# A graph attention layer and a quantised feed-forward layer on one core: edge weights scattered directly, laid over a mask base made on chip

## What is computed

```
w = softplus(edge_type_weights)                      # four numbers
mask = full((N, N), -inf)
mask = mask.at[src, dst].set(w[edge_type - 1])
mask = mask.at[idx, idx].set(where(isneginf(diag), w[3], diag))
scores = einsum('hnd,hmd->hnm', q2, k2) * scale + mask[None]
attn = softmax(scores, axis=-1)
out = einsum('hnm,hmd->hnd', attn, v2) @ wo.T + bo
```

## Time and profile before

| | |
|---|---|
| median of three runs | 340.25 us (337.29 to 341.86) |
| the profiled execution | 339.55 us, of which the span of the trace is 337.6 us |
| TensorE busy | 324.9 us, 96% of the span |
| VectorE, ScalarE, GpSimd busy | 234.8, 182.4, 190.4 us |

### The profile page before, as it was taken

One profiled execution on the slowest core, in us unless ns is written; L12 is line 12 of the kernel. 1 busy time (PEld: TensorE's weight loads), 2 busy tenths in 40 slices (PEclk: granted clock), 3 DMA queues, 4 the chain that ended last, 5 costly groups with the idle time before them and its releaser, 6 DMA issues.

```text
span 337.6 us, 5993 instructions
## 1 busy us (share of the span) xinstructions
PE 324.9 (96%) x2086; PEld 299.0 (89%) x2086; DVE 234.8 (70%) x605; ACT 182.4 (54%) x333; POOL 190.4 (56%) x250
## 2 busy tenths in 40 slices
PE   5999999999999999999799999999999999999995
PEld 5899998878999999999799999999999978888864
DVE  4857887964085554459965979778797876497574
ACT  4824248372843333333147769577595866243572
POOL 6876667446786667489955393755627666100000
PEclk9999999999999999999799999999999999999999
DMA  7997346577053435643230332303113120000005
GB/s 254 371 397 274 122 129 192 183 233 240 7 165 134 128 102 159 217 181 99 90 124 17 112 102 86 124 2 125 61 67 112 57 85 0 0 2 0 2 0 188
DMA packets 17371, 41.72 MB, mean 124 GB/s; under 512 B 3536, under 2 KB 8000, under 8 KB 17344
## 3 DMA queue, kind: packets, MB, share of 16 engines
q1 hardware_dynamic: 14432, 38.87, 33.5%
q0 software_dynamic: 2064, 1.80, 1.9%
q10 hardware_dynamic: 848, 0.70, 0.6%
HBM read 37.99 MB, written 3.37 MB: 123 GB/s over the span
## 4 chain that ended last, share of the span: by engine, by line
PE 57%; DMA 16%; POOL 9%; issue 8%; DVE 7%; ACT 1%; POOLq 0%; DVEq 0%; ACTq 0%
PE PS L749 32%; DMA codes<-ecol,place 14%; POOL codes L436 6%; PE PS L906 5%; PE PS L894 5%; PE PS L882 4%; PE PS L730 3%; PE PS L1041 2%; DMA scratch<-codes 2%; DVE scratch L1304 2%; POOL ring L419 1%; DVE scratch L1303 1%; PE PS L1095 1%; PE PS L818 1%; PE PS L808 1%
## 5 line engine op out<-in xcount | busy, mean ns | idle before, releaser
L419 POOL TENSOR_TENSOR ring<-stage,ring 128x256 fp32r<-128x256 f32 x124 | 97.1, 819 | 38.7 <-ACT ring L502 37.6
L749 PE MATMUL PS<-XT,ring 128*128 128x384 f32 x528 | 93.9, 336 | 0.8 <-DVE QT L1206 0.5
L749 PEld LDWEIGHTS PS<-XT,ring 128*128 128x128 f32 x528 | 91.3, 188 | 1.5 <-issue 0.8
L436 POOL DMA_INDIRECT codes<-ecol,place x51 | 58.3, 1143 | 28.3 <-DMA codes<-ecol,place 16.5
L502 ACT ACTIVATE ring<-stage 128x1024 fp32r<-128x1024 f32 x52 | 54.3, 1056 | 7.0 <-PE PS L749 3.8
L607 ACT ACTIVATE scratch<-scratch,smx 128x384 f32<-128x384 f32 x48 | 28.9, 604 | 22.8 <-DVE smx L1326 22.8
L749 PE MATMUL PS<-QT,ring 128*128 128x384 f32 x192 | 37.2, 349 | 2.1 <-DVE Q L1313 2.1
L749 PEld LDWEIGHTS PS<-QT,ring 128*128 128x128 f32 x192 | 34.7, 196 | 2.7 <-issue 2.7
L1244 DVE TENSOR_TENSOR ring<-stage,ring 128x1024 fp32r<-128x1024 f32 x21 | 25.6, 1225 | 16.3 <-ACT ring L502 16.3
L749 PE MATMUL PS<-AT,ring 128*128 128x384 f32 x192 | 35.2, 338 | 0.0
L749 PEld LDWEIGHTS PS<-AT,ring 128*128 128x128 f32 x192 | 33.0, 188 | 1.5 <-issue 1.5
(11 more groups left out here) (199 smaller groups left out, 476.0 us busy)
## 6 DMA issues: line engine op xcount, KB each, us to landing
stage<-in_weights SPq DMA_DIRECT2D x56, 512.0 KB, 3.4
V<-in_w_gate_up SPq DMA_DIRECT2D x4, 512.0 KB, 3.6
scratch<-codes POOLq DMA_DIRECT2D x3, 576.0 KB, 5.9
X<-in_x SPq DMA_DIRECT2D x3, 512.0 KB, 5.0
out<-X SPq DMA_DIRECT2D x4, 384.0 KB, 2.6
codes<-scratch SPq DMA_DIRECT2D x2, 576.0 KB, 12.9
scratch<-in_w_gate_up SPq DMA_DIRECT2D x2, 512.0 KB, 5.2
V<-in_w_down SPq DMA_DIRECT2D x5, 176.0 KB, 3.7
```

What stands on the lines that cost most here:

```text
L419: ins = pool.tensor_tensor(ring[1][:, slot, piece], stage[:, slot % STAGE, piece], ring[0][:, slot, piece].bitcast(F32), ALU.subtract)
L436: pool.indirect_dma_start(codes[b].rearrange("(n a) -> n a", a=1), bass.IndirectOffsetOnAxis(ap=place[:, t:t + 1], axis=0), ecol[:, VAL, t ...
L749: ins = pe.matmul(outs, lhs[a], rhs[b], start=start and n == 0, stop=stop and n == 2, skip_group_check=True)
```

## The change

The tables are blanked with zeros alone, one broadcast transfer each, so that SyncE issues three transfers in place of nine. Edge values are now the final weights (softplus times 8, at least 1e-30), so that a nonzero bit pattern marks an edge. For that, ScalarE's exp and log move into steps 1 to 3 of the V stage, VectorE's two small operations behind step 5 of that stage (`kind_weights`), and GpSimd selects each edge's weight with four test-and-multiply operations and three additions (`edge_values`) between the low parts of chunks 8 and 9. The four operations that made the codes are gone. In the K stage, VectorE writes the mask's base behind K tile 1 (`edge_base`): -1e30 everywhere, the fourth kind's weight on the diagonal. Each table has its own semaphore when it comes back, and VectorE lays it over the base with one predicated copy (`edges_over`), behind K tiles 4, 5 and 6. The third table comes back into `PT[0][0]`.

```diff
@@ constants, areas @@
+LEAST_WEIGHT = 1e-30
+        tables = [scratch[:, 0:NT * N], scratch[:, NT * N:2 * NT * N],
+                  PT[0][0][:, :, :].rearrange("p t n -> p (t n)").bitcast(F32)]
+        mask_flat = scratch[:, 2 * NT * N:3 * NT * N]
@@ SyncE @@
-            for b in range(1, LISTS):
+            for b in range(LISTS):
                 sp.dma_start(codes[b].rearrange("(m p n) -> p m n", m=NT, p=P), blank.to_broadcast([P, NT, N])
                              ).then_inc(codes_blank[b], 16)
-            sp.wait_ge(diag_ready, 1)
-            for m in range(NT):
...
@@ GpSimd @@
-            chain.step(pool.tensor_scalar(ecol[:, TYP, :], ecol[:, TYP, :], 0.25, 1.0, ALU.mult, ALU.add))
-            for b in range(LISTS):
...
-            ins.then_inc(cols_ready, 1)
+            pool.sem_inc(cols_ready, 1)
+            def edge_values():
+                parts = (VAL, NEG, SPARE, SPARE + 1)
+                pool.wait_ge(kind_ready, 1)
+                for w, to in enumerate(parts):
+                    chain.link(pool.tensor_scalar(ecol[:, to, :], ecol[:, TYP, :], float(w), ew[:, 5, w:w + 1],
+                                                  ALU.is_equal, ALU.mult))
+                chain.join()
+                chain.link(pool.tensor_tensor(ecol[:, VAL, :], ecol[:, VAL, :], ecol[:, NEG, :], ALU.add))
+                chain.step(pool.tensor_tensor(ecol[:, SPARE, :], ecol[:, SPARE, :], ecol[:, SPARE + 1, :], ALU.add))
+                chain.step(pool.tensor_tensor(ecol[:, VAL, :], ecol[:, VAL, :], ecol[:, SPARE, :], ALU.add))
...
-            for c in range(CIV + 2):
+            for c in range(CIV + 1):
                 low(c, c % RING)
+            edge_values()
+            low(CIV + 1, (CIV + 1) % RING)
...
-            for b, area in enumerate((SM[0], SM[1], mask)):
+            for b in range(LISTS):
                 pool.wait_ge(scattered[b], 16 * PER_LIST)
-                pool.dma_start(area, codes[b].rearrange("(m p n) -> p m n", m=NT, p=P)).then_inc(code_back, 16)
+                pool.dma_start(tables[b].rearrange("p (m n) -> p m n", m=NT),
+                               codes[b].rearrange("(m p n) -> p m n", m=NT, p=P)).then_inc(code_back[b], 16)
@@ ScalarE, V stage (the same four lines go from before the Q stage) @@
+                if s == 1:
+                    chain.step(act.activation(ew[:, 1, :], ew[:, 0, :], ACT.Abs))
+                    chain.step(act.activation(ew[:, 2, :], ew[:, 1, :], ACT.Exp, scale=-1.0))
+                elif s == 2:
+                    act.activation(ew[:, 3, :], ew[:, 2, :], ACT.Ln, bias=1.0).then_inc(soft_in, 1)
+                elif s == 3:
+                    act.activation(clip[:, 1, :], clip[:, 0, :], ACT.Exp, scale=-1.0).then_inc(soft_in, 1)
@@ VectorE @@
-            dve.wait_ge(consts, 6)
-            dve.tensor_scalar(diag[:, :], ident[:, :], 1.75, None, ALU.mult).then_inc(diag_ready, 1)
...
+            def kind_weights():
+                dve.wait_ge(soft_in, 1)
+                chain.step(dve.scalar_tensor_tensor(ew[:, 4, :], ew[:, 0, :], 0.0, ew[:, 3, :], ALU.max, ALU.add))
+                dve.tensor_scalar(ew[:, 5, :], ew[:, 4, :], 1.0 / SCALE, LEAST_WEIGHT, ALU.mult, ALU.max
+                                  ).then_inc(kind_ready, 1)
...
+                if s == 5:
+                    kind_weights()
...
+            def edge_base():
+                for b in range(LISTS):
+                    dve.wait_ge(codes_blank[b], 16)
+                dve.wait_ge(kind_ready, 1)
+                chain.link(dve.tensor_scalar(diag[:, :], ident[:, :], 0.0, NO_EDGE, ALU.is_equal, ALU.mult))
+                chain.step(dve.memset(mask_flat, NO_EDGE))
+                for m in range(NT):
+                    chain.link(dve.scalar_tensor_tensor(mask[:, m, m * P:(m + 1) * P], ident[:, :], ew[:, 5, 3:4],
+                                                        diag[:, :], ALU.mult, ALU.add))
+                chain.join()
+
+            def edges_over(b):
+                dve.wait_ge(code_back[b], 16)
+                chain.step(dve.copy_predicated(mask_flat, tables[b].bitcast(I32), tables[b]))
+
             for s in range(5):
                 k_tile(s)
-
-            dve.wait_ge(code_back, 16 * LISTS)
-            chain.step(dve.tensor_tensor(mask, mask, SM[0], ALU.add))
+                if s == 1:
+                    edge_base()
+            edges_over(0)
             k_tile(5)
-            chain.step(dve.tensor_tensor(mask, mask, SM[1], ALU.add))
+            edges_over(1)
             k_tile(6)
-            kind = SM[0].bitcast(I32)
...
-            weight_of(0)
+            edges_over(2)
             k_tile(7)
-            weight_of(1)
-            weight_of(2)
...
             q_low(0)
-            weight_of(3)
             k_low(0)
```

More of the change, by code:

```diff
@@ L215, in gnn_ffn @@
         blank_ready = sem("blank_ready")
-        diag_ready = sem("diag_ready")
+        kind_ready = sem("kind_ready")
         codes_blank = [sem(f"codes_blank{b}") for b in range(LISTS)]
@@ L219, in gnn_ffn @@
         scattered = [sem(f"scattered{b}") for b in range(LISTS)]
-        code_back = sem("code_back")
+        code_back = [sem(f"code_back{b}") for b in range(LISTS)]
         pool_chain = sem("pool_chain")
@@ L396, in _ @@
                                base=-EC, pattern=[[-1, EC]], channel_multiplier=1).then_inc(rows_ready, 1)
-            SRC, DST, KEY, TYP, NEG, VAL = range(6)
+            SRC, DST, KEY, TYP, NEG, VAL, SPARE = range(7)
             pool.wait_ge(edges_in, 2 * 16)
@@ L434, in _ @@
                     else:
-                        pool.wait_ge(codes_blank[b], 16 * (1 if b else 3 * NT - 2))
+                        pool.wait_ge(codes_blank[b], 16)
                     pool.indirect_dma_start(codes[b].rearrange("(n a) -> n a", a=1),
@@ L583, in _ @@
                                        ).then_inc(acc_free, 1)
-            chain.step(act.activation(ew[:, 1, :], ew[:, 0, :], ACT.Abs))
-            chain.step(act.activation(ew[:, 2, :], ew[:, 1, :], ACT.Exp, scale=-1.0))
-            act.activation(ew[:, 3, :], ew[:, 2, :], ACT.Ln, bias=1.0).then_inc(soft_in, 1)
-            act.activation(clip[:, 1, :], clip[:, 0, :], ACT.Exp, scale=-1.0).then_inc(soft_in, 1)
             early(QT, CQ, BIAS_Q)
@@ L1276, in _ @@
             dve.wait_ge(soft_in, 2)
-            chain.step(dve.scalar_tensor_tensor(ew[:, 4, :], ew[:, 0, :], 0.0, ew[:, 3, :], ALU.max, ALU.add))
-            chain.step(dve.tensor_scalar(ew[:, 5, :], ew[:, 4, :], 1.0 / SCALE, None, ALU.mult))
             chain.step(dve.tensor_scalar(clip[:, 2, :], clip[:, 1, :], 1.0, None, ALU.add))
@@ L1288, in k_tile @@
                 tile_low(s + 16, s, s % 2, AT, s + BIAS_K)
+            def edge_base():
[11 more added lines that the diff above has]
+                chain.step(dve.copy_predicated(mask_flat, tables[b].bitcast(I32), tables[b]))
             for s in range(5):
                 k_tile(s)
-            dve.wait_ge(code_back, 16 * LISTS)
-            chain.step(dve.tensor_tensor(mask, mask, SM[0], ALU.add))
+                if s == 1:
+                    edge_base()
+            edges_over(0)
             k_tile(5)
-            chain.step(dve.tensor_tensor(mask, mask, SM[1], ALU.add))
+            edges_over(1)
             k_tile(6)
-            kind = SM[0].bitcast(I32)
-            chain.step(dve.tensor_scalar(kind, mask.bitcast(I32), 21, 3, ALU.logical_shift_right, ALU.bitwise_and))
-            chain.step(dve.tensor_scalar(mask, mask, 0.0, NO_EDGE, ALU.is_equal, ALU.mult))
-            def weight_of(w):
-                chain.step(dve.tensor_scalar(SM[1], kind, kinds[:, w:w + 1], ew[:, 5, w:w + 1], ALU.is_equal, ALU.mult))
-                chain.step(dve.tensor_tensor(mask, mask, SM[1], ALU.add))
-            weight_of(0)
+            edges_over(2)
             k_tile(7)
-            weight_of(1)
-            weight_of(2)
             def q_low(t):
```

13 lines of the change are left out of this document (2 added, 11 removed).

## The result

| | before | changed |
|---|---|---|
| median | 340.30 us (337.29 to 341.88, 6 runs) | 334.67 us (334.56 to 336.96, 6 runs) |
| the profiled execution | 339.55 us, span 337.6 us | 334.56 us, span 332.7 us |
| ratio of times | | 0.990, 95% interval 0.985 to 0.994 |

The forecast was 335.2 us. The ratio is taken over runs of the fast state alone; that of the two medians is 0.983. So the changed kernel is faster by 1.0% or by 1.7%, and both lie inside the 2% that the prediction called no difference.

What follows compares the result with a forecast made beforehand. TensorE, busy 96% of the span, was taken as the bound, so only its waits pay: -4.21 us at the K stage's end, clock included, and -0.5 at the Q tile, -4.7 together. Forecast 335.2 us, range 332.5 to 338.5.

Steps and rivals of the forecast that it cites:

- `q_low(0)`: End of the K stage: TensorE's wait on VectorE before chunk 34 goes, -2.14 us.
- K tile 5: K stage: its low part comes in time after the first copy, so TensorE's wait before chunk 31 goes, -0.33 us.
- The Q wait: Q stage: three table loads leave ScalarE's way to the first Q tile, so TensorE's wait there goes, -0.5 us.
- The clock: Chunk 34: the slow TensorE clock behind the idling goes with the wait, -1.74 us.
- The V stage: Softplus moved there: one ScalarE result 0.6 us late, cost to TensorE 0, at worst 0.2 us.
- The scatters: GpSimd's edge weights ahead of them: first scatter, and by assumption the last and the read-backs, 1.4 us later.
- The cover: K stage: 1.5 us to spare before chunk 31 would wait for late tables.
- GpSimd's pace: Low-part pieces beside the copies take 0.7 to 0.9 us each in place of 1.32; no cost counted.
- The sum: Whole kernel: -4.21 - 0.5 = -4.7 us.
- A: Larger gain, a late scatter chain having cost TensorE all its lateness before: 332 to 333.4 us, chance 0.18.
- B: A late first table makes TensorE wait at chunk 31, or GpSimd stays slow: 336.5 to 339 us, chance 0.16.
- C: Predicated copy far dearer than an addition, TensorE waits at chunks 31 to 34: 350 us, chance 0.02.

Runs made afterwards that it cites:

- (8): Kernel before without the third and fourth kinds' weight pairs in the mask, a shorter VectorE block: 335.85 us, ratio 0.994.
- (3): Changed kernel with five additions of 128x1152 put back behind K tile 7, ahead of `q_low(0)`: 338.36 us, one run.
- (1): Kernel before with only ScalarE's softplus and clip lines moved into the V stage: 337.44 us against 337.60, ratio 0.999.
- (4): Kernel before, nothing changed, traced again: 337.74 us, one run.
- experiment 2: Changed kernel, but VectorE waits for all three tables before its first copy: 339.38 us, ratio to the kernel before 0.998.
- experiment 6: Changed kernel, nothing changed, timed again on another chip: 334.37 us against 337.72 of the kernel before, ratio 0.990.
- 9: Kernel before with softplus and clip moved into the V stage and the third and fourth kinds' weights left out: 335.52 us, ratio 0.992.

## Why the prediction was right

*`q_low(0)`.* Forecast -2.14, measured -2.31 (3.21 - 0.90). Chunk 34 at 161.88, forecast 162.1. The cause is shown by three runs: the block shortened removes the wait (8), a block put back into the changed kernel makes it (3), and tables that came earlier leave it (1).

*K tile 5.* Forecast -0.33, measured -0.61. The copy was priced at 1.9 us; it took 1.82, 2.10 and 1.96. The first began at 145.80, inside 144.6 to 146, and K tile 5 at 147.66, forecast 147.9.

*The Q wait.* Forecast -0.5, measured -0.74. Both short waits cost 0.25 to 0.28 us more than the wait that TensorE's rows show. Part is in how I read the rows: a chunk's row is 4.32 us long, but the next chunk starts 4.16 us after it, so a wait counted from the end of a row is 0.16 us short. The other 0.12 is the chunk behind the wait: 154.47 - 150.19 = 4.28 us in place of 4.16. The same 0.16 is what `q_low(0)` gave above its forecast: TensorE could have had chunk 34 at 158.63 + 4.16 = 162.79, not at 162.95.

*The clock.* Forecast -1.74, measured -1.64. This term was priced rightly and read wrongly: the prediction counted it as given wherever the wait is. That it came in full is luck of the trace that was compared. Experiments 3 and 4 show waits of 2.51 and 1.70 us with no fall, the first trace and experiment 2 waits of 2.14 and 2.57 us with one. So the gain is 3.3 us against a run that kept its clock (337.7 - 334.4, experiment 6), and 5.6 by the medians of the first measurement (340.3 - 334.7), where four of six runs of the kernel before took over 340. The forecast of 4.7 lies between the two. On a chip where the kernel before keeps its clock the same reasoning would have been 1.4 us too high.

*The V stage.* Forecast 0, at worst 0.2; measured +0.45. The opening gives 0.06 of it (13.34 against 13.28), and the softplus itself nothing: the result of chunk 2, forecast 0.6 us late, was taken at 27.78 against 27.70. The rest is the new wait at line 790. TensorE in the kernel before and in the changed one:

```profile
73.82 0.51 PE L783 MATMUL PS<-turner,V 96*128 96x96 f16 x8
```

```profile
74.27 0.52 PE L790 MATMUL PS<-turner,V 96*128 96x96 f16 x8 [0.31 <-DVE V L1242]
```

and VectorE, which prepares these weights, in both:

```profile
70.61 1.22 DVE L1228 TENSOR_REDUCE fsc<-V 128x1 f32<-128x1024 f32 x1 [3.62 <-DMA V<-in_w_down]
```

```profile
71.06 1.22 DVE L1233 TENSOR_REDUCE fsc<-V 128x1 f32<-128x1024 f32 x1 [3.38 <-DMA V<-in_w_down]
```

VectorE waits for a load of feed-forward weights, which SyncE issued at 66.86 and 66.92. From issue to VectorE's start it took 3.75 us before and 4.14 in the changed kernel. In the 14 traces the wait at this line stands exactly in the five in which this took 4.13 to 4.52 us, and in none of the nine in which it took 3.40 to 3.93; the changed kernel has both (3.64 in experiment 6). So the forecast looked in the wrong place: it weighed ScalarE's results, and the cost came from a load. Whether the change makes that load slower stays open: all five are among the ten traces with the moved softplus. Four of these ten, experiments 1, 3 and 9 among them, also have a wait of 0.4 us at the keys' transposes, and none of the four without it.

*The scatters.* Forecast 1.4 us later, measured 2.0: `edge_values` took the 2.9 us and the wait 0.41 that were forecast, and chunk 9's low part took 3.28 us in place of 2.83. The first read-back is 3.0 us later than before, the third only 1.0. The cover took it all.

*GpSimd's pace.* Forecast 0.7 to 0.9 us a piece, measured 0.93, enough: no wait of TensorE on it before the scores.

*The sum.* -0.61 - 2.31 - 0.74 - 1.64 + 0.45 = -4.85, forecast -4.7. The short waits erred by 0.5 and `q_low(0)` by 0.2 one way, the V stage by 0.45 and the clock by 0.1 the other. That they cancel is luck; the waits, their places and what removes them were forecast.

*The rivals.* A gave a large gain to a late scatter chain. Its spread was real, and the traces give it another cause: the clock (4). The landing was the same in two traces whose times differ by 1.8 us (4), and an earlier one moved `q_low(0)` little (1). A much later landing is in no trace of the kernel before, so what it would do stays untested. B's wait is real when it is provoked (2); the changed order kept clear of it. C fell with the first copy's 1.82 us. The changed kernel has a second level of its own, 336.8 and 337.0 in two of six runs at a mean clock of 0.998 and 1.000. It is not the clock, none of those runs was traced, and it stays open.

## What to carry to other kernels

When an in-order engine works through a long block that another engine wants only the end of, look at what it waits for inside the block: the length behind the last such wait is what pays, and an earlier start upstream may be absorbed there. Price a wait of the matmul engine with and without the clock that may fall behind it, and give both: two medians of one kernel that differ by 1% may be one time with and one without the fall. Measure what a wait costs from the start of one block of matmuls to the start of the next, not by the idle time alone. And where several transfers end one after another, give each its own semaphore: waiting for all together took most of this gain back in three of five runs.

## What the runs showed of the hardware

**An issue of a scatter is stretched by an addition.** In GpSimd's timeline of the changed kernel the issue at 134.89 took 1.90 us, the next ones 0.97. VectorE's timeline has beside it

```profile
134.72 1.23 DVE L1249 TENSOR_TENSOR ring<-stage,ring 128x1024 fp32r<-128x1024 f32 x1 [0.33 <-ACT ring L507]
```

As in the earlier trace rows, the issue ends 0.84 us after the addition does (135.95 and 136.79). In the kernel before, 12 of the 51 issues are lengthened so by 0.15 us or more; they start while such an addition runs. Those of the changed kernel beside the fill at 130.55 and the three small operations at 131.60 are not: 0.97 us each. The prediction had feared the latter. The Trainium skill (SBUF — State Buffer, Who interferes with whom) infers that such an addition leaves descriptor generation alone; these rows speak against it. By the same section of the Trainium skill an operation with two SBUF inputs contends with GpSimd's reads, and there the trace agrees: pieces of 0.71 us alone took 1.32 beside the wide block and 0.93 beside three copies.

**The clock's fall is not decided by the length of the wait alone.** Waits of 1.70 and 2.51 us kept it, 2.14, 2.57, 3.40, 3.56 and 6.10 us lost it, and by the mean clocks of its runs (0.992 to 1.000 in experiment 6) the kernel before does both from run to run. Behind the waits of 2.14 and 2.57 us the fall cost 1.64 and 1.68 us.
